# A decoder layer on one NeuronCore: values ahead of context pieces, head loads behind the stores, and the last attention batch in order of readiness

## The chip, the cores and the metric

The kernel runs on one core of a Trainium2 chip. The time is the device time of one execution in microseconds (us), a median over runs. The profile is one execution of the same kernel. The engines are TensorE (PE; its weight loads PEld), VectorE (DVE), ScalarE (ACT), GpSimd (POOL) and SyncE (SP), which here only issues the DMAs. Each engine runs its own instructions in program order and waits on semaphores.

## What is computed

One post-norm decoder layer, float32, for 8 batches of 128 rows with 512 columns (inputs `x`, a context of the same shape, and a mask):

```
x = layernorm(x + out(softmax(q k / 4 + alibi, causal) v))          # self-attention, 32 heads of 16
x = layernorm(x + wo(softmax(rope(q) rope(k) / sqrt(128) + mask) v)) # cross-attention, 32 query heads, 8 key/value heads of 128
x = layernorm(x + ffn(x))
ffn(x) = layernorm(relu(x up)^2 down + ((x fc1) expert fc2) * (sum of the 2 largest of x gate)) * gamma + beta
```

## The kernel before

**Precision.** Every float32 operand of a large product is split into a rounded part "hi" (a copy on ScalarE) and the rest "lo" (a subtraction, on GpSimd or VectorE), and `product` (L34) makes three matmul passes, hi·hi, hi·lo, lo·hi. A 128x512 tile with a contraction over 512 is 12 matmuls.

**Weights** come in pieces of 128x512 through a ring of five slots, `stage`: SyncE loads a slot (`Ring.load`), ScalarE makes hi (L162), GpSimd makes lo (L167), and the next load into that slot waits for that lo (`s_lo`).

**Four stages follow one another**, each with a function for each engine in steps `n`:

- `ProjectSelf` (A): 24 tiles in `order`: 16 query/key tiles ("qk", 0 to 15) and 8 value tiles ("v", 16 to 23), in four PSUM banks; a bank is free again when VectorE has added the bias into `val` (`s_val`). For each tile ScalarE makes hi (`s_vhi`) and GpSimd lo (`s_vlo`). SyncE stores the qk tiles in DRAM and loads them back by heads (`heads.load`, 12 DMAs for 16 heads of one batch). The same engines split the eight pieces of the transposed context `ctx` (numbers 20 to 27), one with each value tile: ScalarE `piece_hi` (L321), VectorE `piece_lo` (L378).
- `AttendSelf` (B): 64 steps of attention over four heads each, plus `STEPS - NS` = 7 steps that run the pipeline out. Beside it, steps 0 to 63 project the cross-attention's keys and values from the context into `kv_d` (`project`, with `pj` banks 6 and 7). For each batch there is a chain, the closing: weighted values in `ov` -> parts added (L837) -> times `rden` (L598, `s_o`) -> transposed on TensorE (L786) -> hi, lo (`oT`) -> output product (`close`, `s_y`) -> residual added (L866, `s_z`) -> `Rows.statistics` -> `Rows.root` and the normalisation (L108, L114, `s_row`) -> transposed (L122) -> hi (L132), lo (L137) into `xT`. `closing(n, lag, ends)` gives the batch that a part works on in step n; `ends` lists the steps for the last batches, 6 and 7. In the steps from 60 on, the first pieces of the cross-attention's weights (`NEXT_LOAD`, `NEXT_SPLIT`; 0 to 3 query weights, 4 to 7 `wo`) and the first four query tiles (`QUERY`, `ROTATE`) are worked in.
- `AttendCross` (C): 64 steps. Step n projects and rotates query tile n+5, computes scores n, transposes n-2, outputs n-3 and values n-2. The rotation is three VectorE instructions (`rotate`, L1098 to L1100), a sum on GpSimd (L1161), a hi on ScalarE (L976), a lo on GpSimd (L1169).
- `FeedForward` (D): its weight pieces are split within C's steps 58 to 64 (`SPLIT`), the two `lat` tiles (expert times fc2) are made at step `LAT`, and `x` of batch b gets statistics, normalisation (GpSimd, L114) and transposes at steps 59+b, 60+b, 61+b. From step `FIRST` = 65 on the `up` tiles begin.

The order of each engine's work is written out by hand; nothing reorders it.

## Time and profile before

| | |
|---|---|
| median of 3 runs | 978.54 us (976.09 to 979.15) |
| the profiled execution | 979.14 us; its span 977.4 us |
| TensorE busy in the span | 911.4 us (93%) |
| VectorE, GpSimd, ScalarE busy | 672.1, 526.4, 499.5 us |
| mean granted TensorE clock | 0.975 of 2.4 GHz |

The span runs from the first to the last instruction; the other 1.7 us of the execution lie around it. A share of busy time is a mean over stages with different limits, so the stages' borders have to be looked at by themselves.

### The profile page before, as it was taken

To read this page: it belongs to the slowest core of one execution; us is meant where nothing else is said; L and a number is where in the kernel's file an instruction comes from. 1 tells how busy PE (TensorE), PEld (TensorE's weight loads), DVE (VectorE), ACT (ScalarE), POOL (GpSimd) and SP (SyncE) were. 2 spreads that over 40 slices of the span, in tenths; PEclk is the share of its full clock that TensorE was granted. 3 is DMA by queue.
4 is the path that set the end of the run, shared out by engine and by line. 5 is a ranking of instruction groups with operands and counts; after the bars stand their busy time and mean duration, and the time that the engine had idled before them with its cause. 6 is when DMAs were issued, how large, how long until landed. Compare 5 with 4: busy or idle time off the path is not lost.

```text
span 977.4 us, 15760 instructions
## 1 busy us (share of the span) xinstructions
PE 911.4 (93%) x4812; PEld 772.1 (79%) x4812; DVE 672.1 (69%) x2163; ACT 499.5 (51%) x1565; POOL 526.4 (54%) x446
## 2 busy tenths in 40 slices
PE   7994999999999677999999999999999998999996
PEld 6873888888888556888888888888888887787885
DVE  5444777777777446777777777777777776665646
ACT  4324977776777215545554555455545554450220
POOL 4534753353235556666666666666666677655101
PEclk9997999999999878999999999999999998999999
DMA  8794995585454521113031121312113112110001
GB/s 273 232 234 129 220 181 148 135 156 133 132 130 141 197 94 33 33 36 127 33 119 37 53 107 33 122 41 79 73 36 127 34 35 85 55 33 22 22 6 38
DMA packets 68371, 96.65 MB, mean 99 GB/s; under 512 B 7232, under 2 KB 44352, under 8 KB 67264
## 3 DMA queue, kind: packets, MB, share of 16 engines
q1 hardware_dynamic: 68288, 95.65, 34.3%
q8 instruction: 39, 0.64, 0.3%
q14 instruction: 44, 0.36, 0.2%
HBM read 68.33 MB, written 27.26 MB: 98 GB/s over the span
## 4 chain that ended last, share of the span: by engine, by line
PE 77%; issue 6%; ACT 5%; DVE 5%; POOL 4%; SPq 1%; DMA 1%; POOLq 0%; ACTq 0%; DVEq 0%
PE banks L34 60%; PE banks L1055 4%; PE banks L1035 3%; PE banks L778 3%; PE banks L737 2%; ACT B_prob L663 2%; PE banks L736 2%; PE banks L1056 2%; SPq L209 1%; PE banks L766 1%; POOL x L1571 1%; PE banks L122 1%; POOL C_t L1161 1%; DMA stage<-ctxT_dram 1%; DVE A_val L392 1%
## 5 line engine op out<-in xcount | busy, mean ns | idle before, releaser
L34 PE MATMUL banks<-C_wo,C_o 128*128 128x512 f32 x768 | 191.4, 398 | 1.6 <-DVE C_o L1148 1.0
L34 PE MATMUL banks<-xT,C_w 128*128 128x512 f32 x768 | 191.0, 399 | 1.5 <-DVE xT L137 1.5
L34 PEld LDWEIGHTS banks<-xT,C_w 128*128 128x128 f32 x768 | 148.2, 194 | 33.2 <-issue 1.9
L34 PEld LDWEIGHTS banks<-C_wo,C_o 128*128 128x128 f32 x768 | 140.4, 189 | 29.7 <-issue 1.2
L976 ACT ACTIVATE C_q<-C_t 128x512 fp32r<-128x512 f32 x64 | 40.5, 633 | 175.6 <-POOL C_t L1161 175.6
L663 ACT ACTIVATE B_prob<-B_prob,B_top 128x128 f32<-128x128 f32 x256 | 99.5, 392 | 33.4 <-DVE B_top L816 32.5
L1169 POOL TENSOR_TENSOR C_q<-C_t,C_q 128x512 fp32r<-128x512 f32 x64 | 82.7, 1293 | 47.6 <-ACT C_q L976 47.6
L985 ACT ACTIVATE C_prob<-C_prob,C_top 128x128 f32<-128x128 f32 x256 | 99.0, 392 | 2.4 <-DVE C_top L1119 2.4
L1161 POOL TENSOR_TENSOR C_t<-C_t,C_t 128x512 f32<-128x512 f32 x64 | 82.8, 1294 | 13.6 <-DVE C_t L1100 13.4
L1055 PE MATMUL banks<-C_kv,C_q 128*128 128x256 f32 x256 | 68.8, 346 | 4.1 <-issue 3.7
L167 POOL TENSOR_TENSOR C_wo<-stage,C_wo 128x512 fp32r<-128x512 f32 x32 | 41.1, 1285 | 56.6 <-ACT C_wo L162 56.6
L1177 POOL TENSOR_TENSOR C_prob<-C_prob,C_rden 128x512 f32<-128x512 f32 x64 | 66.6, 1041 | 8.4 <-DVE C_rden L1130 8.4
L167 POOL TENSOR_TENSOR C_w<-stage,C_w 128x512 fp32r<-128x512 f32 x32 | 41.2, 1286 | 54.5 <-ACT C_w L162 54.5
L816 DVE CUSTOM_DVE_ANT_0 B_prob<-banks,causal 128x128 f32<-128x128 f32 x256 | 58.9, 287 | 12.0 <-issue 11.2
L1002 ACT ACTIVATE C_o<-banks 128x512 fp32r<-128x512 f32 x64 | 38.3, 599 | 53.5 <-PE banks L34 53.5
L1098 DVE TENSOR_TENSOR C_t<-banks,trig 128x512 f32<-128x512 f32 x64 | 44.2, 691 | 28.8 <-PE banks L34 28.7
L1148 DVE TENSOR_TENSOR C_o<-banks,C_o 128x512 fp32r<-128x512 f32 x64 | 44.3, 692 | 26.9 <-ACT C_o L1002 26.9
L822 DVE TENSOR_TENSOR B_pT<-banks,B_pT 128x512 fp32r<-128x512 f32 x64 | 44.1, 689 | 24.2 <-ACT B_pT L646 24.1
L1119 DVE CUSTOM_DVE_ANT_0 C_prob<-banks,C_prob 128x128 f32<-128x128 f32 x256 | 58.9, 286 | 2.7
L34 PE MATMUL banks<-C_pT,C_kv 128*128 128x512 f32 x192 | 54.8, 394 | 5.4 <-DVE C_pT L1137 5.0
L737 PE MATMUL banks<-vhl,B_pT 128*128 128x16 f32 x256 | 59.2, 256 | 0.0
L1056 PE MATMUL banks<-C_kv,C_q 128*128 128x128 f32 x256 | 57.6, 225 | 0.0
(154 smaller groups left out, 2137.0 us busy)
## 6 DMA issues: line engine op xcount, KB each, us to landing
C_kv<-cross_kv_d SPq DMA_DIRECT2D x8, 2048.0 KB, 8.5
cross_kv_d<-B_k_out SPq DMA_DIRECT2D x16, 512.0 KB, 2.7
cross_kv_d<-B_v_out SPq DMA_DIRECT2D x16, 512.0 KB, 4.1
stage<-wq_dram SPq DMA_DIRECT2D x32, 256.0 KB, 2.6
stage<-wo_dram SPq DMA_DIRECT2D x32, 256.0 KB, 2.6
heads_q<-heads_q_d SPq DMA_DIRECT2D x96, 64.0 KB, 4.0
heads_k<-heads_k_d SPq DMA_DIRECT2D x96, 64.0 KB, 4.1
heads_q_d<-cT SPq DMA_DIRECT2D x8, 512.0 KB, 2.6
```

The source lines that it names most:

```text
L34: mm = eng.matmul(out, stationary[i], moving[j], start=first and n == 0, stop=last and n == len(PASSES) - 1)
L167: eng.tensor_tensor(out, self.stage[:, n % self.SLOTS, :], hi.bitcast(F32), ALU.subtract).then_inc(self.s_lo, 1)
L663: last = eng.activation(e, e, ACT.Exp, bias=self.top[:, n % 4, h:h + 1], scale=-1.0, accum_out=self.total[:, HG * G + h:HG * G + h + 1])
L737: mm = eng.matmul(out[:, at:at + DH], self.pT[1][:, m % 2, h * S:(h + 1) * S], v[:, 0:DH], start=False, stop=True)
L816: last = eng.tensor_tensor_reduce(self.prob[:, n % 3, h * S:(h + 1) * S], self.sc[n % 2][:, h * S:(h + 1) * S], self.heads.causal, 1.0, 3e ...
L985: last = eng.activation(e, e, ACT.Exp, bias=self.top[:, n % 2, h:h + 1], scale=-1.0, accum_out=self.total[:, n % 2, h:h + 1])
L1055: eng.matmul(out, q[0][:, h, tok], both, start=True, stop=False)
L1056: mm = eng.matmul(out[:, 0:S], q[1][:, h, tok], both[:, 0:S], start=False, stop=True)
L1119: last = eng.tensor_tensor_reduce(self.prob[:, n % 2, h * S:(h + 1) * S], self.sc[:, h // 2, h % 2, 0, :], self.prob[:, n % 2, h * S:(h + ...
L1161: eng.tensor_tensor(t1, t1, t2, ALU.add).then_inc(self.s_sum, 1)
L1169: eng.tensor_tensor(self.query(r, 1), by_batch(self.t1[:, r % 2, :]), self.query(r, 0).bitcast(F32), ALU.subtract).then_inc(self.s_qlo, 1)
L1177: eng.tensor_tensor(e, e, self.rden[:, (n - 1) % 2, :].unsqueeze(2).broadcast_to([P, self.Q, S]), ALU.mult).then_inc(self.s_norm, 1)
```

## The change

It has four groups of edits.

1. **Values ahead of context pieces.** For a value tile, VectorE now adds the bias and ScalarE makes hi before the context piece of that tile is split, and not behind it. TensorE's first step of B and the first key projection no longer wait for all 24 `val`; only the first value projection (f == 1) does.
2. **Heads loads behind the stores.** Batch 0's head loads, which stood behind the stores of tiles 10 and 12, stand behind the last store; context pieces 20 to 23 are loaded behind the stores of tiles 9, 11, 13 and 15, pieces 24 to 27 between the two head loads.
3. **The last batch in order of readiness.** From step 65 on VectorE has its own list, `vector_end`. `root` is called by itself; the normalisation of batches 6 and 7 and the last scaling by `rden` move from GpSimd to VectorE. Several `ends` are one step earlier. Pieces 4 to 7 of the cross-attention's weights are split at step 70, behind all the rest of B, and `EARLY` is 9 (pieces 9 and 10 are loaded by C). In C's steps 0 to 2 the query projection stands ahead of the value product.
4. **Feed-forward pieces one step forward.** `SPLIT` begins at step 57, `LAT` is 59.

The diff, cut to its core (the bodies of `minima`, `turned_lo`, `add_parts`, `output_lo` and `add_row` are the old pieces of `vector` as functions):

```diff
@@ -109,7 +109,6 @@
 
     def normalise(self, eng, b):
 
-        self.root(eng, b)
         eng.wait_ge(self.s_rstd, b + 1)
         eng.tensor_scalar(self.x[:, b, :], self.x[:, b, :], self.moments[:, b, 0:1], self.rstd[:, b:b + 1],
                           ALU.subtract, ALU.mult).then_inc(self.s_row, 1)
...
-    HEADS = (10, 12)
 
     pieces = [(kind, c, 0) for c in range(C) for kind in ("x", "w")] + \
...
             heads.store(eng, i, m, h, self.tiles[i % heads.RING])
-            if i in self.HEADS:
-                heads.wait_stored(eng, self.QK // 2)
-                heads.load(eng, 0, self.HEADS.index(i))
-            if i >= self.QK - C:
-                self.load_piece(eng, self.CONTEXT + i - self.QK + C)
+            if i >= self.QK // 2 and i % 2 == 1:
+                self.load_piece(eng, self.CONTEXT + (i - self.QK // 2) // 2)
+        heads.wait_stored(eng, self.QK // 2)
+        heads.load(eng, 0, 0)
         for n in range(self.CONTEXT + C, len(self.pieces)):
             self.load_piece(eng, n)
+        heads.load(eng, 0, 1)
         for n in range(Ring.SLOTS):
             eng.wait_ge(self.s_lo, max(j for j in range(len(self.pieces)) if j % self.RING == n) + 1)
             ring.load(eng, n, sources[n])
@@ -322,9 +320,10 @@
 
     def scalar_tile(self, eng, i):
 
-        for n in self.pieces_with(i):
-            self.piece_hi(eng, n)
         kind, m, h = self.order[i]
+        if kind == "qk":
+            for n in self.pieces_with(i):
+                self.piece_hi(eng, n)
         eng.wait_ge(self.s_val, i + 1)
         src = self.val[:, i % 2, :]
...
             src = src.rearrange("p (h d) -> p h d", d=DH)
         eng.activation(dst, src, ACT.Copy).then_inc(self.s_vhi, 1)
+        if kind == "v":
+            for n in self.pieces_with(i):
+                self.piece_hi(eng, n)
 
     def scalar(self, eng):
 
...
@@ -380,9 +382,10 @@
 
     def vector_tile(self, eng, i):
 
-        for n in self.pieces_with(i):
-            self.piece_lo(eng, n)
         kind, m, h = self.order[i]
+        if kind == "qk":
+            for n in self.pieces_with(i):
+                self.piece_lo(eng, n)
         eng.wait_ge(self.s_acc, i + 1)
...
         else:
             eng.tensor_scalar(out, acc, self.bqk[:, m:m + 1], None, ALU.add).then_inc(self.s_val, 1)
+        if kind == "v":
+            for n in self.pieces_with(i):
+                self.piece_lo(eng, n)
 
     def vector(self, eng):
 
...
 
-    NEXT_LOAD = {57: range(5), 62: (5, 6), 64: (7,), 67: (8,), 68: (9,), 69: (10,)}
-    NEXT_SPLIT = {60: 0, 61: 1, 62: 2, 65: 3, 66: 4, 67: 5, 68: 6, 69: 7}
+    NEXT_LOAD = {57: range(5), 62: (5, 6), 64: (7,), 67: (8,)}
+    NEXT_SPLIT = {60: (0,), 61: (1,), 62: (2,), 65: (3,), 70: (4, 5, 6, 7)}
     QUERY = {64: 0, 65: 1, 66: 2, 67: 3}
     ROTATE = {65: 0, 66: 1, 67: 2, 68: 3}
 
...
-        return self.closing(n, 8 + 4 * half, ((56, 64), (60, 67))[half])
+        return self.closing(n, 8 + 4 * half, ((56, 64), (60, 66))[half])
...
+    def scale(self, eng, b, half):
+
+        done = 2 * b + half + 1
+        wait(eng, self.s_o, done - 1)
+        eng.wait_ge(self.s_oadd, done)
+        eng.wait_ge(self.s_rden, done)
+        o = self.o[:, 16 * half:16 * half + 16, :]
+        eng.tensor_tensor(o, o, self.rden[:, 16 * half:16 * half + 16].unsqueeze(2).broadcast_to([P, 16, DH]),
+                          ALU.mult).then_inc(self.s_o, 1)
+
 
     def gpsimd_pieces(self, eng, n):
 
@@ -590,22 +606,19 @@
 
         for half in range(2):
             b = self.half_of(n, half)
-            if b is not None:
-                done = 2 * b + half + 1
-                eng.wait_ge(self.s_oadd, done)
-                eng.wait_ge(self.s_rden, done)
-                o = self.o[:, 16 * half:16 * half + 16, :]
-                eng.tensor_tensor(o, o, self.rden[:, 16 * half:16 * half + 16].unsqueeze(2).broadcast_to([P, 16, DH]),
-                                  ALU.mult).then_inc(self.s_o, 1)
+            if b is not None and n <= self.NS:
+                self.scale(eng, b, half)
         j = self.tile("k", n, 2)
         if j is not None:
             eng.wait_ge(self.s_khi, j + 1)
             out = self.k_out[j % 2]
             eng.tensor_tensor(out[:, :, 1, :], by_batch(self.t1[j % 2][:, :]), out[:, :, 0, :].bitcast(F32),
                               ALU.subtract).then_inc(self.s_klo, 1)
-        b = self.closing(n, 19, (65, 69))
+        b = self.closing(n, 19, (64, 69))
         if b is not None:
-            self.rows.normalise(eng, b)
+            self.rows.root(eng, b)
+            if n < self.NS:
+                self.rows.normalise(eng, b)
         j = self.tile("k", n, 1)
         if j is not None:
             eng.wait_ge(self.s_cos, j + 1)
...
             eng.wait_ge(self.s_x[b], 16)
             eng.tensor_tensor(self.x1[:, b, :], self.x1[:, b, :], self.bout[:, :], ALU.add).then_inc(self.s_xadd, 1)
-        if n in self.NEXT_SPLIT:
-            self.cross.piece_lo(eng, self.NEXT_SPLIT[n])
+        for i in self.NEXT_SPLIT.get(n, ()):
+            self.cross.piece_lo(eng, i)
         if n in self.ROTATE:
             self.cross.tile_sum(eng, self.ROTATE[n])
             self.cross.tile_lo(eng, self.ROTATE[n])
...
             eng.activation(self.pT[0][:, n % 2, :], self.tp, ACT.Copy).then_inc(self.s_phi, 1)
-        b = self.closing(n, 21, (66, 70))
+        b = self.closing(n, 21, (65, 70))
         if b is not None:
             self.rows.hi(eng, b)
...
             eng.activation(self.k_out[j % 2][:, :, 0, :], by_batch(self.t1[j % 2][:, :]), ACT.Copy).then_inc(self.s_khi, 1)
         self.scalar_pieces(eng, n)
-        if n in self.NEXT_SPLIT:
-            i = self.NEXT_SPLIT[n]
+        for i in self.NEXT_SPLIT.get(n, ()):
             if i == 3:
...
         if part == 0:
-            if f < 2:
+            if f == 1:
                 eng.wait_ge(self.before.s_val, len(self.before.order))
-            else:
+            elif f > 1:
...
             if n == 0:
-                eng.wait_ge(self.before.s_val, len(self.before.order))
...
             mm.then_inc(self.s_ot, 1)
-        b = self.closing(n, 20, (66, 69))
+        b = self.closing(n, 20, (65, 69))
         if b is not None:
             if b == B - 1:
...
-        b = self.closing(n, 18, (65, 69))
+        b = self.closing(n, 18, (64, 69))
         if b is not None:
-            eng.wait_ge(self.s_y, b + 1)
-            eng.wait_ge(self.s_xadd, b + 1)
-            row = self.x1[:, b, :]
-            eng.tensor_tensor(row, self.yb, row, ALU.add).then_inc(self.s_z, 1)
-            eng.wait_ge(self.s_z, b + 1)
-            self.rows.statistics(eng, b)
-        if n in self.ROTATE:
-            if self.ROTATE[n] == 0:
-                for s in (self.s_klo, self.s_vlo):
-                    eng.wait_ge(s, len(self.FILL) // 2)
-            self.cross.rotate(eng, self.ROTATE[n])
+            self.add_row(eng, b)
+
+    def vector_end(self, eng):
+
+
+
+        first, last = B - 2, B - 1
+        self.rows.normalise(eng, first)
+        for s in (self.s_klo, self.s_vlo):
+            eng.wait_ge(s, len(self.FILL) // 2)
+        self.cross.rotate(eng, 0)
+        self.turned_lo(eng, self.NS - 1)
+        self.rows.lo(eng, first)
+        self.cross.rotate(eng, 1)
+        self.add_parts(eng, last, 1)
+        self.scale(eng, last, 1)
+        self.output_lo(eng, last)
+        self.cross.rotate(eng, 2)
+        self.cross.rotate(eng, 3)
+        self.add_row(eng, last)
+        self.rows.normalise(eng, last)
+        self.rows.lo(eng, last)
 
 
 class AttendCross:
...
     PIECES = 2 * HG * NG
-    EARLY = 11
+    EARLY = 9
     STEPS = NS + 3
...
-    SPLIT = {58: (0, 1), 59: (2, 3), 60: (4, 5), 61: (6, 7), 62: (8, 9), 63: (10, 11), 64: (12,)}
+    SPLIT = {57: (0, 1), 58: (2, 3), 59: (4, 5), 60: (6, 7), 61: (8, 9), 62: (10, 11), 63: (12,)}
     DOWN = 13
     STATS, NORMAL, TURN, TAKE = 59, 60, 61, 62
-    LAT = 60
+    LAT = 59
     FIRST = 65
 
     tiles = [("lat", l, 0) for l in range(L)] + \
...
         if self.NORMAL <= n < self.NORMAL + B:
+            self.rows.root(eng, n - self.NORMAL)
             self.rows.normalise(eng, n - self.NORMAL)
         for i in self.SPLIT.get(n, ()):
             self.piece_lo(eng, i)
...
         for n in range(self.before.STEPS, self.NORMAL + B):
+            self.rows.root(eng, n - self.NORMAL)
             self.rows.normalise(eng, n - self.NORMAL)
         for m in range(self.M):
...
                 d.tensor_between(eng, n)
+                if n < 3:
+                    c.queries(eng, n)
                 c.values(eng, n)
-                c.queries(eng, n)
+                if n >= 3:
+                    c.queries(eng, n)
                 d.tensor_behind(eng, n)
             d.tensor(eng)
 
         @block.vector
         def _(eng):
             a.vector(eng)
-            for n in range(b.STEPS):
+            for n in range(b.NS + 1):
                 b.vector(eng, n)
+            b.vector_end(eng)
             for n in range(c.STEPS):
                 d.vector_ahead(eng, n)
                 c.vector(eng, n)
...
```

## Rows read from the trace of the kernel before

**Rows 1.** Busy time of each engine in four stretches, with granted clock and DMA share
```profile
77.00:87.00 10.00, 0.37 (x3) 0.10 (x1) 6.20 (x7) 3.57 (x7) 3.80 (x3) 0.73 0.27 79
...
333.00:353.00 20.00, 11.78 (x41) 9.36 (x41) 7.80 (x14) 4.42 (x9) 13.26 (x11) 0.70 0.46 166
...
373.00:795.00 422.00, 422.00 (x2185) 357.86 (x2184) 325.43 (x1008) 218.27 (x674) 270.07 (x224) 1.00 0.19 65
795.00:845.00 50.00, 43.50 (x219) 36.10 (x218) 34.81 (x111) 26.48 (x80) 41.15 (x34) 0.93 0.27 80
```

**Rows 2.** Timeline at the end of A: start, us, engine, line, operation, count, idle before
```profile
54.65 9.13 PE L34 MATMUL banks<-A_w,A_xT 128*128 128x512 f32 x39 [0.24 <-DVE A_w L378]
...
56.65 0.43 SPq L275 DMA_DIRECT2D stage<-ctxT_dram  x1
...
62.66 0.63 ACT L321 ACTIVATE cT<-stage 128x512 fp32r<-128x512 f32 x1 [6.74 <-DMA stage<-ctxT_dram]
...
63.94 0.68 DVE L392 TENSOR_TENSOR A_val<-banks,A_bv 128x512 f32<-128x512 f32 x1
...
65.84 1.38 DVE L378 TENSOR_TENSOR cT<-A_rest,cT 128x512 fp32r<-128x512 f32 x1 [1.22 <-ACT cT L321]
...
86.17 0.68 DVE L392 TENSOR_TENSOR A_val<-banks,A_bv 128x512 f32<-128x512 f32 x1
...
86.90 0.80 PE L766 MATMUL banks<-heads_k,heads_q 128*128 128x256 f32 x2 [9.63 <-DVE A_val L392]
90.22 2.90 PE L34 MATMUL banks<-cT,B_wk 128*128 128x512 f32 x6 [2.53 <-POOL B_wk L167]
```

**Rows 3.** Timeline of TensorE from the end of B into C
```profile
325.54 0.63 PE L122 MATMUL banks<-ident,x 128*128 128x128 f32 x4 [1.57 <-issue]
...
335.10 1.11 PE L786 MATMUL banks<-ident,B_o 128*128 128x128 f32 x4 [6.19 <-POOL B_o L598]
335.87 5.39 PE L34 MATMUL banks<-xT,C_w 128*128 128x512 f32 x12
...
347.62 0.36 PE L1055 MATMUL banks<-C_kv,C_q 128*128 128x256 f32 x1 [3.65 <-issue]
...
352.92 8.16 PE L34 MATMUL banks<-xT,C_w 128*128 128x512 f32 x24 [1.50 <-DVE xT L137]
...
371.46 1.62 PE L34 MATMUL banks<-C_pT,C_kv 128*128 128x512 f32 x3 [4.95 <-DVE C_pT L1137]
```

**Rows 4.** Timeline of GpSimd in the same stretch
```profile
346.25 1.27 POOL L1169 TENSOR_TENSOR C_q<-C_t,C_q 128x512 fp32r<-128x512 f32 x1 [0.74 <-ACT C_q L976]
...
348.14 2.08 POOL L114 TENSOR_SCALAR x<-x,first_moments,first_rstd 128x512 f32<-128x512 f32 x1
```

**Rows 5.** The page's costliest groups: count, then busy us, mean ns of one
```profile
L976 ACT ACTIVATE C_q<-C_t 128x512 fp32r<-128x512 f32 x64 | 40.5, 633 | 175.6 <-POOL C_t L1161 175.6
...
L1169 POOL TENSOR_TENSOR C_q<-C_t,C_q 128x512 fp32r<-128x512 f32 x64 | 82.7, 1293 | 47.6 <-ACT C_q L976 47.6
...
L1161 POOL TENSOR_TENSOR C_t<-C_t,C_t 128x512 f32<-128x512 f32 x64 | 82.8, 1294 | 13.6 <-DVE C_t L1100 13.4
...
L1177 POOL TENSOR_TENSOR C_prob<-C_prob,C_rden 128x512 f32<-128x512 f32 x64 | 66.6, 1041 | 8.4 <-DVE C_rden L1130 8.4
...
L1098 DVE TENSOR_TENSOR C_t<-banks,trig 128x512 f32<-128x512 f32 x64 | 44.2, 691 | 28.8 <-PE banks L34 28.7
```

**Rows 6.** Groups by shape, VectorE: a normalisation of D as VectorE does it
```profile
L1513 DVE TENSOR_SCALAR x<-x,D_moments,D_rstd 128x512 f32<-128x512 f32 x8 | 4.4, 546 | 5.3 <-POOL D_rstd L1574 5.3
```

**Rows 7.** Timeline of TensorE where C runs out and D begins
```profile
819.89 1.11 PE L122 MATMUL banks<-ident,x 128*128 128x128 f32 x4 [4.02 <-DVE D_lat L1466]
...
823.25 4.12 PE L34 MATMUL banks<-C_wo,C_o 128*128 128x512 f32 x12
...
835.90 2.97 PE L34 MATMUL banks<-C_wo,C_o 128*128 128x512 f32 x12 [1.03 <-DVE C_o L1148]
...
844.23 3.00 PE L34 MATMUL banks<-xT,D_up 128*128 128x512 f32 x12
```

More of the change, by code:

```diff
@@ L802, in tensor, with minima, turned_lo, add_parts @@
             self.cross.project(eng, self.QUERY[n])
+    def minima(self, eng, n):
+        if n == 0:
+            eng.wait_ge(self.heads.s_causal, 2)
+        eng.wait_ge(self.s_sc, n + 1)
+        wait(eng, self.s_tp, n - 2)
+        wait(eng, self.s_exp, n - 3)
+        eng.memset(self.carrier[:, n:n + 1], 0.0)
+        for h in range(HG):
+            last = eng.tensor_tensor_reduce(
+                self.prob[:, n % 3, h * S:(h + 1) * S], self.sc[n % 2][:, h * S:(h + 1) * S],
+                self.heads.causal, 1.0, 3e38, ALU.add, ALU.min, self.top[:, n % 4, h:h + 1])
+        last.then_inc(self.s_top, 1)
+    def turned_lo(self, eng, m):
+        eng.wait_ge(self.s_phi, m + 1)
+        eng.tensor_tensor(self.pT[1][:, m % 2, :], self.tp, self.pT[0][:, m % 2, :].bitcast(F32),
+                          ALU.subtract).then_inc(self.s_plo, 1)
+    def add_parts(self, eng, b, half):
+        o = self.o[:, 16 * half:16 * half + 16, :]
+        eng.wait_ge(self.s_olow, 2 * b + half + 1)
+        eng.tensor_tensor(o, self.values_of(half)[:, :, 0, :], o, ALU.add).then_inc(self.s_oadd, 1)
+    def output_lo(self, eng, b):
+        eng.wait_ge(self.s_ohi, b + 1)
+        eng.tensor_tensor(self.oT[1][:, :, :], self.ot.rearrange("p (c s) -> p c s", c=C),
+                          self.oT[0][:, :, :].bitcast(F32), ALU.subtract).then_inc(self.s_olo, 1)
+    def add_row(self, eng, b):
+        eng.wait_ge(self.s_y, b + 1)
+        eng.wait_ge(self.s_xadd, b + 1)
+        row = self.x1[:, b, :]
+        eng.tensor_tensor(row, self.yb, row, ALU.add).then_inc(self.s_z, 1)
+        eng.wait_ge(self.s_z, b + 1)
+        self.rows.statistics(eng, b)
     def vector(self, eng, n):
@@ L808, in vector @@
         if self.live(n):
[L809 to L819 removed]
+            self.minima(eng, n)
         if self.live(n, self.LT):
[L821 to L824 removed]
+            self.turned_lo(eng, n - self.LT)
+        b = self.closing(n, 21, ())
         if b is not None:
@@ L834, in vector @@
             if b is not None:
[L835 to L837 removed]
+                self.add_parts(eng, b, half)
         b = self.closing(n, 15, (63, 67))
         if b is not None:
[L840 to L842 removed]
+            self.output_lo(eng, b)
         cos, sin = (self.trig[:, 2 + i, :].unsqueeze(1).broadcast_to([P, 4, S]) for i in range(2))
```

21 lines of the change are left out of this document (removed).

## The prediction

> **What bounds the kernel now.** I read the windows first. Through C's steady part TensorE is busy 422.0 of 422.0 us at the full clock [rows 1], so nothing can be won there. What can be won lies at the borders of stages: 9.6 of 10 us idle at the end of A, 8.2 of 20 at the end of B at a mean clock of 0.70, and 6.5 of 50 at 0.93 where C runs out [rows 1]. The timeline then says what ends each wait. End of A: TensorE has done its last value tile at 77.27 (86.90 less 9.63) and waits for the last `val` on VectorE; then 2.53 us more for the first key weight [rows 2]. End of B: 6.19 us for the scaled output of batch 7, 3.65 us ahead of the first scores, 1.50 us for the last transposed row, 4.95 us for the first value product [rows 3]. Each long gap is followed by slow work: a projection of 12 matmuls takes 5.39 us at 335.87 [rows 3], and the stream of 39 in 9.13 us at 54.65 [rows 2] makes 2.7 to 2.8 of it; that is the lower of the two clocks, 1.2 instead of 2.4 GHz. C to D: 4.02 us for `lat` [rows 7].
>
> **Part 1, end of A.** VectorE is the bound: its `val` of the first value tile comes at 63.94, because ScalarE had to wait until 62.66 for a context piece whose load was issued at 56.65, behind the head loads; the eighth `val` comes at 86.17 [rows 2]. So a tile costs (86.17 - 63.94)/7 = 3.18 us, and TensorE needs only 2.7. The cycle is `val` 0.68, hi 0.63, piece hi about 0.6, piece lo 1.38 [rows 2], and each waits for the one before. Turning the order round doesn't shorten it: the same four stand in the same circle. What it does is let it start: the first value tile is complete about 55.4 (54.65 plus three matmuls), and its `val` needs no context any more. First `val` 55.5, eighth 55.5 + 7 x 3.18 = 77.7 instead of 86.17: 8.5 us earlier. Behind the eighth there is now a last piece lo, up to 81.0; the key weight's hi follows the last piece hi at about 79.7 and GpSimd's lo ends about 81.7, where it ended just ahead of 90.22 [rows 2]. So the first key projection starts at 81.8 and not 90.2: 8.4 us. The first scores move ahead to 74.9 and wait for nothing but their heads. Against this stand the loads: SyncE now issues piece 23, twelve head loads, pieces 24 to 27 and twelve more behind the last store at 57.3. In before a piece issued at 56.65 was in use 6.0 us later, in just such a queue [rows 2]. Piece 24 would be issued about 64 and arrive about 70 to 71.5; the cycle wants it at 69.5. Lower bound of the gain: 2 us late there and 1 us for the key weight, 5.4 us; upper bound 8.5. I take 7.5, one microsecond late. The batch's second heads are wanted only four steps later. The low clock at the first steps of B costs now as before, since TensorE still idles nearly 7 us.
>
> **Part 2, end of B.** I walk the chain with the durations of [rows 4, 5, 6]. The normalisation of batch 6 moves to VectorE (0.55 us [rows 6] instead of 2.08 [rows 4]) and comes right behind its output product, so that its transposes stand one step earlier and TensorE runs through without the gap of 1.57 us ahead of its transposes: it has the third query tile done at 327.3 instead of 328.9 (335.10 less 6.19 [rows 3]). Meanwhile the last parts are added and scaled on VectorE behind the second rotation (about 325.1 + 0.4 + 0.4), so the output transposes find their input at 326.0: the 6.19 us go, and the fourth query tile runs at the full clock, 2.7 for 5.39. The output product of batch 7 ends about 333.3, not 344.0 (347.62 less 3.65 [rows 3]). What is late next is the rotations: VectorE does the third and fourth behind `output_lo` (329.3), 3 x 0.7 each, to 333.5; the residual and statistics follow to 335.4. GpSimd and ScalarE need 1.29 + 0.63 + 1.29 and some 0.1 for hand-overs, 3.3 us a tile, for tiles 2 and 3: 331.4 + 6.7 = 338.1 [rows 5]; that lo ended at 347.52 before (346.25 + 1.27 [rows 4]). Then root 0.6 (347.52 to 348.14) and normalisation 0.55 to 339.3 (350.22 before [rows 4]), while the scores run from 338.1; transposes, hi and lo put C's first projection at 342.4 against 352.92 [rows 3]: 10.5 us. TensorE idles nearly 5 us ahead of the scores, so I let the pair of projections cost the 8.16 us that it cost [rows 3], at the low clock in its first half. In C's step 2 the fourth projection, 2.7 us, now stands in the 4.95 us gap ahead of the value product, and neither is slowed by it (the product took 1.62 us for three matmuls [rows 3]); after taking off 1.2 us that the next value product waits for its own lo, this adds 2.3. Sum 12.8, of which I take 12.5. The four splits of `wo` at step 70 occupy GpSimd for 4 x 1.29 = 5.2 us from about 342.3 to 347.5, and the sum of the fifth query tile is ready about then: hidden, but without slack; if it loses, 1 to 2 us. Bounds: below, 8 (one more wait of 2 us in VectorE's single file, and the low clock over one more projection, 2.7); above, 14.5 (the clock stays up ahead of C, which takes 2.7 off the pair of projections, less what the chain then waits for).
>
> Two vector operations of two SBUF inputs or in a fast mode now run beside GpSimd. The piece lo takes 1.38 us at 65.84 beside GpSimd and 0.69 without it [rows 2] (the multiplication of as many elements shows the 0.69 [rows 5]). I take 0.3 us for the scaling and nothing for the normalisations, since GpSimd has nothing to do at those moments. The Trainium skill (SBUF — State Buffer, Who interferes with whom) says why: VectorE in a two-port mode or with two SBUF inputs and a reading GpSimd shut each other out for a whole instruction. By that rule each of three moved instructions could wait or hold up a full GpSimd instruction, and part 2 would give some 3 us less; the trace agrees about the piece lo and can't show the moved ones.
>
> **Part 3, C to D.** The third piece that `lat` needs was split at step 59; at step 58 GpSimd has the same two-piece room. `lat` (12 matmuls, 2.7 us) then stands at step 59 and its hi and lo are done by about 815.1 instead of 819.8, when TensorE gets to the first transposes of the second norm: the 4.02 us go [rows 7]. So does the low clock behind them: the output product took 4.12 us for 2.97 [rows 7], and a mean clock of 0.93 over 50 us [rows 1] is 3.5 us of lost clock, of which I put 0.8 into the idle time and 2.7 into work. The later steps are held by GpSimd, which has 1.04 [rows 5] + 0.6 + 2.08 [rows 4] + 2 x 1.29 = 6.3 us a step while pieces last, and TensorE has about 5.3; the pieces now end a step earlier, so that the waits there, 1.03 before 835.90 [rows 7] and the rest of the 6.5 us idle [rows 1], can go too. 6.5 + 2.7 = 9.2; the first `up` tile would start at 835 and not 844.23. I take 8.5; lower bound 4 (one wait comes back and the clock falls again), upper 9.2. From there to the end the order is the old one and TensorE sets it: the gain stays.
>
> **Sum.** 7.5 + 12.5 + 8.5 = 28.5 us. The profiled execution's own 979.14 less this is 950.6; the median shown is 0.6 lower, so 950.0.
>
> **Rivals.** *The tail of B stays at the low clock* or VectorE's single file (`vector_end` puts some ten jobs in one fixed order) meets a wait that I don't see, or each of its three moved instructions loses a GpSimd instruction of 1.3 us as the piece lo does [rows 2]. For it: gaps of 3.65 us and more were each followed by slow matmuls [rows 3], and the new gap is nearly 5. Against: the biggest gap is gone. Part 2 gives 5: 957. The Trainium skill (TensorE: Matmul & The Clock Gate, What's actually happening) says that the slow state is the default and activity releases it; the trace agrees [rows 3]. *The loads decide at the end of A*: context piece 24 or the key weight comes 5 us late behind 24 head loads. Part 1 gives 2: 955.5. *C to D is held by GpSimd all the same*, as its 6.3 us a step suggest; part 3 gives 3: 955.5. *The change does nothing where it counts*: the first part's circle of four is as long as before, and if TensorE at the start of B were held by the weights' arrival in every case, part 1 gives 0 and the others half: 968; still faster. *The other side*: TensorE falls to 1.2 GHz over whole stretches of the transitions because the small gaps now follow one another. Each slow 12-matmul tile costs 2.7 us more [rows 3], so it decides once 28.5/2.7, some 11, are slow beyond those that are slow now. From B's step 64 to C's step 2 there are ten (eight queries, two output products), about three of them slow now, and C's last steps hold six more. The trace shows no stretch of dense work that stays slow, so 2 in 100.
>
> **How the numbers follow.** The forecast 0.60, with its own range of 946 to 955. Part 2 short 0.15, loads 0.09, GpSimd in part 3 0.10, little or nothing 0.04, slower 0.02. The range takes in the two bounds that are added (upper 8.5 + 14.5 + 9.2 = 32.2, so 946; lower 5.4 + 8 + 4 = 17.4, so 961). A difference under 0.3% (2.9 us) is about what a measurement of this kernel can't tell from none. Faster 0.95, same 0.02, slower 0.03.
>
> **What would show it.** Right: the first key projection at about 82 to 83 with a gap of some 7 us ahead; the output transposes of batch 7 without a gap, C's first projection about 18 us earlier than 352.92 and C's steady part about 20 us earlier; the gap before the first D transpose gone, the first `up` tile 28 us earlier, clock 1.00 there. Wrong: a wait of ScalarE for a context piece over 2 us, the first scores of B waiting for heads, more than 6 us idle on TensorE ahead of C's first scores, a clock of 0.5 in C's steps 2 and 3, or GpSimd releasing the first transposes of D.

## The result and the profile after

The changed kernel takes 953.81 us (median of 4 runs, 952.4 to 954.57) beside 978.85 for the kernel before on the same chip: ratio 0.9748, 95% interval 0.9726 to 0.977, so 25.0 us less. Forecast were 950.0, with bounds that give 946 to 961. The profiled executions differ by more, 952.4 and 979.14, 26.7 us. One execution of the same code is not the next: in three traces with the same A (before, tail_only and ff_only below) the first value product starts at 54.65, 54.18 and 54.75, and the first key projection 35.6, 34.6 and 34.6 us behind it. The one microsecond more in the trace of before is ScalarE's wait for the first context piece: 6.74 us there, 5.81 and 5.75 in the other two. So I compare marks within a trace and take whole runs for the verdicts.

The windows of the changed kernel: stretch, length, busy us of TensorE, its weight loads, VectorE, ScalarE and GpSimd, then granted clock, DMA share, GB/s.

```profile
76.00:84.00 8.00, 0.77 (x2) 0.71 (x3) 4.38 (x13) 3.97 (x11) 4.20 (x3) 0.71 0.65 134
326.00:336.00 10.00, 3.75 (x14) 3.27 (x15) 4.13 (x13) 3.12 (x7) 5.46 (x5) 0.63 0.07 29
336.00:346.00 10.00, 10.00 (x43) 8.07 (x41) 6.14 (x21) 2.55 (x10) 6.98 (x7) 0.86 0.32 107
360.00:776.00 416.00, 416.00 (x2157) 352.91 (x2156) 322.63 (x1002) 217.05 (x672) 270.57 (x224) 1.00 0.19 67
776.00:818.00 42.00, 38.79 (x209) 32.00 (x208) 33.11 (x108) 23.76 (x72) 37.12 (x31) 1.00 0.27 83
```

C's steady part is as full as before [rows 1]; what changed are the borders. At the end of B two gaps are left, 4.79 and 1.50 us, with a mean clock of 0.63 in the ten microseconds around them, and where C runs out 3.2 us are idle in place of 6.5.

The timeline at the end of A, to be laid beside [rows 2]:

```profile
56.25 0.69 DVE L395 TENSOR_TENSOR A_val<-banks,A_bv 128x512 f32<-128x512 f32 x1 [0.40 <-PE banks L34]
...
63.52 0.63 ACT L336 ACTIVATE vhl<-A_val 128x512 fp32r<-128x512 f32 x1 [2.04 <-DVE A_val L395]
64.06 0.62 ACT L319 ACTIVATE cT<-A_rest 128x512 fp32r<-128x512 f32 x1
...
64.71 1.37 DVE L380 TENSOR_TENSOR cT<-A_rest,cT 128x512 fp32r<-128x512 f32 x1 [1.22 <-ACT cT L319]
66.00 0.68 DVE L395 TENSOR_TENSOR A_val<-banks,A_bv 128x512 f32<-128x512 f32 x1
...
78.72 0.68 DVE L395 TENSOR_TENSOR A_val<-banks,A_bv 128x512 f32<-128x512 f32 x1
...
83.23 2.90 PE L34 MATMUL banks<-cT,B_wk 128*128 128x512 f32 x6 [7.73 <-POOL B_wk L166]
```

The first bias waits for TensorE alone; from there on bias, copy of the value, copy of the piece, low part and next bias follow one another every 3.2 us, none of them behind a DMA.

TensorE from the end of B into C, beside [rows 3]:

```profile
319.87 0.60 PE L797 MATMUL banks<-ident,B_o 128*128 128x128 f32 x4
320.23 3.01 PE L34 MATMUL banks<-xT,C_w 128*128 128x512 f32 x12
323.08 2.88 PE L34 MATMUL banks<-B_wout,B_oT 128*128 128x512 f32 x12
330.75 0.55 PE L1102 MATMUL banks<-C_kv,C_q 128*128 128x256 f32 x1 [4.79 <-issue]
...
335.06 7.44 PE L34 MATMUL banks<-xT,C_w 128*128 128x512 f32 x24 [1.50 <-DVE xT L136]
...
347.82 2.98 PE L34 MATMUL banks<-xT,C_w 128*128 128x512 f32 x12
352.93 0.93 PE L34 MATMUL banks<-C_pT,C_kv 128*128 128x512 f32 x3 [2.14 <-DVE C_pT L1184]
```

The 6.19 us are gone, the fourth query tile takes 3.01 and not 5.39. GpSimd in the same stretch, beside [rows 4], shows what is late next:

```profile
329.39 1.26 POOL L1216 TENSOR_TENSOR C_q<-C_t,C_q 128x512 fp32r<-128x512 f32 x1 [0.74 <-ACT C_q L1023]
330.61 0.55 POOL L108 TENSOR_TENSOR first_rstd<-first_moments,power 128x1 f32<-128x1 f32 x1
```

TensorE where C runs out, beside [rows 7]:

```profile
794.77 0.94 PE L34 MATMUL banks<-C_pT,C_kv 128*128 128x512 f32 x3 [1.05 <-ACT C_pT L1041]
...
800.82 0.93 PE L34 MATMUL banks<-C_pT,C_kv 128*128 128x512 f32 x3 [0.22 <-issue]
...
809.17 3.00 PE L34 MATMUL banks<-C_wo,C_o 128*128 128x512 f32 x12 [0.98 <-DVE C_o L1195]
...
814.32 3.01 PE L34 MATMUL banks<-C_wo,C_o 128*128 128x512 f32 x12 [0.59 <-issue]
...
817.52 3.00 PE L34 MATMUL banks<-xT,D_up 128*128 128x512 f32 x12
```

The 4.02 us and the slow output product are gone, but the 1.03 and 0.59 us of before stand as 0.98 and 0.59, and 1.05 us at 794.77 is new.

The same end of C, from the transposes of step 59 to the first `up` tile, in the trace before, in the changed kernel and in the run `piece_copies_behind` below:

```profile
797.86:844.23 46.37, 39.87 (x203) 33.15 (x202) 32.80 (x107) 23.95 (x71) 37.52 (x32) 0.93 0.28 82
776.81:817.52 40.71, 37.50 (x203) 30.96 (x202) 32.45 (x107) 22.95 (x69) 35.83 (x30) 1.00 0.28 85
775.95:814.97 39.02, 37.32 (x203) 30.92 (x202) 32.14 (x107) 23.32 (x69) 34.82 (x30) 1.00 0.29 89
```

TensorE's idle time (length less its busy time) goes from 6.50 to 3.21 us, its busy time from 39.87 to 37.50.

From these marks the 26.7 us divide: up to B's last scores (307.31 before, 300.12 after) 7.2; from there to the transposes of C's step 59 (797.86 and 776.81) 13.9; from there to the first `up` tile (46.37 and 40.71) 5.7.

### The profile page after: what moved, and what is told of

Same layout as the page of the kernel before. It is cut to its first block, busy times and chain, and to the rows that moved or that the text cites. A ratio compares the mean times of both kernels' runs of the same rounds, so it can differ in the third digit from the quotient of the medians.

```text
span 950.6 us, 15757 instructions
## 1 busy us (share of the span) xinstructions
PE 901.9 (95%) x4812; PEld 765.9 (81%) x4812; DVE 673.7 (71%) x2166; ACT 498.4 (52%) x1565; POOL 522.3 (55%) x443
## 4 chain that ended last, share of the span: by engine, by line
PE 79%; ACT 6%; issue 6%; DVE 6%; POOL 2%; DMA 0%; POOLq 0%; ACTq 0%; DVEq 0%
PE banks L34 61%; PE banks L1102 4%; PE banks L1082 3%; PE banks L789 3%; PE banks L749 2%; ACT B_prob L676 2%; PE banks L748 2%; PE banks L1103 2%; PE banks L777 1%; POOL x L1620 1%; PE banks L121 1%; ACT C_prob L1032 1%; DVE A_val L395 1%; ACT cT L319 0%; DVE B_prob L825 0%
## 5 line engine op out<-in xcount | busy, mean ns | idle before, releaser
L34 PE MATMUL banks<-xT,C_w 128*128 128x512 f32 x768 | 186.9, 393 | 1.5 <-DVE xT L136 1.5
L34 PEld LDWEIGHTS banks<-xT,C_w 128*128 128x128 f32 x768 | 145.0, 190 | 32.0 <-issue 1.9
L34 PE MATMUL banks<-cT,B_wk 128*128 128x512 f32 x192 | 52.4, 409 | 7.9 <-POOL B_wk L166 7.7
```

The costliest lines, as they stand in the source:

```text
L34: mm = eng.matmul(out, stationary[i], moving[j], start=first and n == 0, stop=last and n == len(PASSES) - 1)
```

## Experiments

Each run was measured beside the kernel before on its own chip, whose median was 978.4 to 978.9 us; the ratios are to that. The edits are shown shortened, with words in brackets for code left out.

### Each part alone, on the kernel before

`loads_only` takes over the order of the loads alone (group 2 of the change):

```diff
@@ ProjectSelf.sync @@
-            if i in self.HEADS: (wait, heads.load)
-            if i >= self.QK - C: self.load_piece(...)
+            if i >= self.QK // 2 and i % 2 == 1:
+                self.load_piece(eng, self.CONTEXT + (i - self.QK // 2) // 2)
+        heads.load(eng, 0, 0); pieces 24 to 27; heads.load(eng, 0, 1)
```

> The kernel before with the order of the loads alone changed: pieces 20 to 23 go out between the last eight stores, the loads of the heads behind the stores, the rest between the two. Theory one, the order of the loads carries most of part 1: the value tile waited for late context pieces, and with them earlier the last value tile comes at about 80.2 us and the first k projection at about 84.2 instead of 90.22, so about 6 us off. Rival, the order of the work carries it: each piece is still split ahead of its value tile, so the chain of piece, value tile, piece stays as it was and under 2 us come off.

972.86 us, ratio 0.9943 (0.9928 to 0.9958), 5.6 us. Its first key projection starts at 84.17, forecast 84.2.

`order_only` has the other half, values ahead of pieces and the loosened waits:

```diff
@@ ProjectSelf.scalar_tile and vector_tile @@
-        for n in self.pieces_with(i): piece        # ahead of the bias or copy, for every tile
+        (that for "qk" tiles; for "v" tiles the same loop behind it)
```

> The kernel before with only the order of work at the end of A changed (value tile ahead of its context piece on ScalarE and VectorE, and the waits of the first scores and projections on the value tiles loosened); the loads stay as before. Theory one: a piece that lands late still holds the value tile behind it, so about 3 us come off, and loads and order together (7.2) are less than the sum of each alone (6 + 3). Rival, the order carries it: 6 to 7 us.

976.15 us, 0.9975 (0.9964 to 0.9986), 2.4 us by the runs; the key projection comes at 85.90. VectorE's biases, and ScalarE's copy of the first piece between them:

```profile
55.46 0.69 DVE L397 TENSOR_TENSOR A_val<-banks,A_bv 128x512 f32<-128x512 f32 x1 [0.39 <-PE banks L34]
...
61.02 0.63 ACT L321 ACTIVATE cT<-stage 128x512 fp32r<-128x512 f32 x1 [4.20 <-DMA stage<-ctxT_dram]
...
62.29 0.69 DVE L397 TENSOR_TENSOR A_val<-banks,A_bv 128x512 f32<-128x512 f32 x1
```

The first bias is early, the second comes 6.8 us later, behind the first piece, whose copy on ScalarE waited for its load. So it is the loads that carry most of part 1, and the two halves share one wait. Counted from the first value product to the first key projection it is 34.6 us in tail_only and ff_only, 31.4 with the order alone, 29.6 with the loads alone and 28.0 with both: 3.2, 5.0 and 6.6 us off.

`tail_only` is the third group of edits alone (separate `root`, `vector_end`, steps 64 to 70, `wo` at step 70, queries first in C's steps 0 to 2).

> The kernel before with the end of B alone changed (the last batch in order of readiness, steps 64 to 70, and the queries of C's first three steps ahead of the values). From the two traces part 2 is 13.9 us; if the parts are independent this run is 13.9 off (ratio 0.9858). Rival, a share of it was the earlier arrival of loads or a clock that part 1 set: 12 or less. The first projection of C at about 342 in this trace.

964.29 us, 0.9855 (0.984 to 0.987), 14.2 us. From B's last scores to C's first projection it takes 34.99 us, the changed kernel 34.94, before 45.61. In this trace the end of B needs nothing of the other parts.

`ff_only` is `SPLIT` and `LAT` alone, the fourth group.

> The kernel before with the feed-forward pieces and the latent tiles one step forward and nothing else. If the parts add, 5.7 us come off (ratio 0.9942), as between the traces of before and after. Rival, the forecast's 8.5 was right and 2.8 of it was eaten by an interplay with the other parts: then 8.5 here. In the trace, TensorE still waits for C_pT and C_o in steps 61 to 64.

974.05 us, 0.995 (0.9935 to 0.9965), 4.9 us; from step 59's transposes to the first `up` tile 40.72 us, the changed kernel's 40.71. So the 2.8 us that the forecast had more weren't lost to the other parts. The four ratios added make 27.1 us, and the whole change, by its ratio, 24.7; what is left between them is the overlap of the first two. By the runs the order adds nothing to the loads that can be told (24.7 less 14.2 and 4.9 is 5.6, as much as the loads alone); by the marks above it adds 1.6.

### Parts of the end of B, on the changed kernel

`no_swap`:

```diff
-                if n < 3: c.queries(eng, n)
                 c.values(eng, n)
-                if n >= 3: c.queries(eng, n)
+                c.queries(eng, n)
```

> The changed kernel with the queries of C's steps 0 to 2 behind the values again. Theory: the values of steps 2 wait for the split of the transposed probabilities, and the projection that stands ahead of them covers that wait; without it TensorE stands still and the rotation of the next query tile starts later: 2.3 to 3.2 us slower than the changed kernel (about 956.5). Rival: GpSimd's file of rotations, splits and normalisations sets the steps there, and the place of the projection on TensorE changes nothing (953.8).

956.09 us, 0.9776 (0.9761 to 0.9792), 2.7 us more than the changed kernel by the ratios, whose intervals just touch; in the trace the stretch from C's first projection to the first `up` tile is 485.85 us for 482.46, 3.4 more. The old wait is back, with its low clock:

```profile
353.26 1.62 PE L34 MATMUL banks<-C_pT,C_kv 128*128 128x512 f32 x3 [4.95 <-DVE C_pT L1184]
354.68 5.08 PE L34 MATMUL banks<-xT,C_w 128*128 128x512 f32 x12
```

The swap is worth part of the wait that it covers (2.14 us of it are left) and the slow projection behind it: by the trace more than the forecast's 2.3.

`spread` splits `wo` one a step again, and with it loads pieces 9 and 10 in B again (`NEXT_LOAD` and `EARLY` as before the change):

```diff
-    NEXT_SPLIT = {60: (0,), 61: (1,), 62: (2,), 65: (3,), 70: (4, 5, 6, 7)}
+    NEXT_SPLIT = {60: (0,), 61: (1,), 62: (2,), 65: (3,), 66: (4,), 67: (5,), 68: (6,), 69: (7,)}
```

> The changed kernel with the four output weights of C split one a step in steps 66 to 69 again, as before the change, in place of all four in step 70. Theory: four low parts of 1.26 us stand in GpSimd's file among the sums and low parts of the queries, of which 2 to 4 us fall on the way to the first scores (330.75): 2.5 to 4 us slower than the changed kernel. Rival: GpSimd's gaps of 0.74 to 2.00 us between its rotations hold them, since it waits for the copy on ScalarE and the rotation on VectorE: under 1 us.

954.56 us, 0.9761 (0.9746 to 0.9775): by the runs not to be told from the changed kernel. In the trace the first scores come 33.10 us behind B's last scores, in place of 30.63, so 2.5 us late, and all of it arrives at the first `up` tile (2.7); its opening of A happened to be 0.8 us earlier. The trace speaks for the theory, the runs leave anything from nothing to some 3 us, and the two later loads aren't told apart from the splits.

`root_first` takes up the two rows of GpSimd above: the root's input is there at 327.98 (VectorE's last step of the statistics ends then), but it stands behind the low part of query tile 3.

```diff
             self.cross.tile_sum(eng, self.ROTATE[n])
+            if self.ROTATE[n] == 3: self.rows.root(eng, B - 1)
             self.cross.tile_lo(eng, self.ROTATE[n])
@@ AttendSelf.tensor @@
-            if b == B - 1: self.cross.scores(eng, 0)
             eng.wait_ge(self.s_z, b + 1)
             self.rows.transpose(eng, b)
+            if b == B - 1: self.cross.scores(eng, 0)
```

> The changed kernel with the square root of the last row's variance ahead of the low part of query tile 3 in GpSimd's file (its input is there at 327.98, it ran at 330.61), and the transposes of that row ahead of C's first scores on TensorE. Theory: the row is normalised at about 329.2 in place of 331.19, its low part done at about 332.3 in place of 334.92, and C's first projection starts at about 332.6 in place of 335.06: 2.4 us faster (951.4). Rival: the projections of C's steps 0 to 2 wait for something else (the rotation, GpSimd) and catch nothing: under 0.5 us.

949.26 us, 0.9705 (0.969 to 0.972). From B's last scores to C's first projection 32.62 us, 2.3 less, and 0.5 more behind it: 2.9 us in the trace, 4.2 by the ratios of the runs. The edit has two halves, and the rows of the changed kernel show that the root alone could not have done it: there the row is normalised at 331.74 (VectorE from 331.19, 0.55), but the transposes stand behind the scores, which fill TensorE until 332.49.

```profile
331.19 0.55 DVE L113 TENSOR_SCALAR x<-x,first_moments,first_rstd 128x512 f32<-128x512 f32 x1 [3.21 <-POOL first_rstd L108]
...
332.49 1.07 PE L121 MATMUL banks<-ident,x 128*128 128x128 f32 x4
```

In `root_first` they start at 330.06, the scores run behind them, and the pair of projections waits for nothing. What each half is worth alone wasn't run.

`warm` fills TensorE's two gaps with products that nothing reads:

```diff
+        if n == 0: (30 products heads_q x heads_k, 128x512, into the bank of the first projection)
+            if b == B - 1: (20 products of xT, 128x512, into a free bank, ahead of C's first scores)
```

> The changed kernel with products added that nothing reads, in the two gaps of TensorE's: 30 of 512 columns ahead of B's first k projection, 20 ahead of C's first scores. Theory: the granted clock stays at its upper level where the rows show the lower one (0.50 in 80 to 86 and in 330 to 338), the scores, transposes and first projections behind the gaps run in half the time, and some 3.4 us at the end of B and 1.5 us at the end of A come off. Rival: what stands behind the gaps waits for VectorE, ScalarE and GpSimd again, and the faster products only make longer waits: under 1 us together.

948.94 us, 0.9695 (0.9673 to 0.9718): by the ratios 5.2 us less than the changed kernel, give or take 3, and 2.6 between the two profiled executions, which is what the marks divide. By the marks: the key projection starts at 83.22 as before and takes 1.62 us for six matmuls in place of 2.90, B's last scores come 1.3 us earlier; at the end of B it is 1.0 to C's first projection and 0.3 behind it. That is 1.3 for the 1.5 expected at A and 1.3 for the 3.4 at B. The windows show why:

```profile
330.00:331.00 1.00, 1.00 (x10) 0.90 (x9) 0.52 (x1) 0.00 (x0) 0.00 (x0) 1.00 0.00 0
331.00:332.00 1.00, 0.25 (x3) 0.01 (x1) 0.08 (x1) 0.71 (x2) 0.00 (x0) 1.00 0.00 0
332.00:333.00 1.00, 0.24 (x1) 0.28 (x2) 1.00 (x3) 1.00 (x3) 0.52 (x1) 0.68 0.00 0
333.00:334.00 1.00, 1.00 (x3) 0.81 (x4) 0.96 (x9) 0.96 (x2) 1.00 (x2) 0.50 0.00 0
```

The scores and transposes ran at the full clock, but the wait of 1.50 us for the last row's low part stayed, the clock fell within it (0.68 on the mean of the microsecond from 332, with the projections starting at 332.76), and the pair of projections took 7.13 us, nearly the 7.44 of the changed kernel.

### The end of A

`late_low_part` opens the circle:

```diff
@@ ProjectSelf.vector_tile @@
-        if kind == "v": low parts of pieces_with(i)
+        if kind == "v" and i > self.QK: low parts of pieces_with(i - 1)
@@ vector @@
+        (behind the loop: low parts of pieces_with of the last tile)
```

> The changed kernel with VectorE's low part of a context piece behind the bias of the next value tile, in place of ahead of it. Theory: the period of 3.19 us of the value tiles is a circle (bias on VectorE 0.68, copy of the value tile on ScalarE, copy of the piece, low part 1.37, next bias); broken, TensorE's 2.76 us a tile sets the period, the last bias comes at about 75.6 in place of 78.72 and B's first k projection at about 80.1 in place of 83.23: 3.1 us off. Rival: pieces 24 to 27 (issued 65.1 to 67.3, landed up to 73.8) hold it then, and about 1 us comes off.

951.19 us, 0.9723 (0.9696 to 0.975), which the runs alone don't tell from the changed kernel. The period is TensorE's 2.72 us, and the last bias comes at 74.64:

```profile
69.20 0.69 DVE L395 TENSOR_TENSOR A_val<-banks,A_bv 128x512 f32<-128x512 f32 x1 [1.43 <-PE banks L34]
70.08 0.69 DVE L380 TENSOR_TENSOR cT<-stage,cT 128x512 fp32r<-128x512 f32 x1 [0.18 <-ACT cT L319]
71.92 0.69 DVE L395 TENSOR_TENSOR A_val<-banks,A_bv 128x512 f32<-128x512 f32 x1 [1.15 <-PE banks L34]
...
76.55 1.34 DVE L380 TENSOR_TENSOR cT<-stage,cT 128x512 fp32r<-128x512 f32 x1 [0.62 <-ACT cT L319]
```

but the first key projection came at 81.31, only 1.3 us earlier when the 0.66 us of the earlier opening are taken off. SyncE and ScalarE say why:

```profile
73.40 0.43 SPq L156 DMA_DIRECT2D stage<-wk_dram  x1
...
79.19 0.63 ACT L161 ACTIVATE B_wk<-stage 128x512 fp32r<-128x512 f32 x1 [2.67 <-DMA stage<-wk_dram]
```

The key weight stood behind twelve head loads in SyncE's queue. It arrived after the last bias had long been done. A context piece was late too, as the rival had it (ScalarE waited 1.57 us for it at 69.41), but the biases kept their period. Neither theory had the weight: the circle was real, and right behind it stood another queue.

### Where C runs out

`light_pieces` takes GpSimd's work away:

```diff
@@ FeedForward.piece_lo, for the pieces ahead of `down` @@
-        self.ring.lo(eng, self.first + n, hi[:, :], lo[:, :])
+        (the same subtraction for one column; the products read hi in the place of lo)
```

> The changed kernel, with the low parts of the 13 feed-forward pieces of steps 57 to 63 left out: GpSimd computes one column of each, and the products read the high part twice (same work on TensorE, another result). That takes 13 x 1.25 = 16 us from GpSimd. Theory one, GpSimd's file of 6.2 us a step (normalise 793.43, 799.65, 805.86) holds steps 61 to 64: TensorE's idle 3.2 us between 776 and 818 goes down to about 1 and 2 to 2.5 us come off. Rival, the circle of values, output copy on ScalarE, low part on VectorE and outputs holds them: the waits of 0.98 for C_o at 809.17 and 0.59 at 814.32 stay, and under 0.5 us come off.

951.91 us, 0.9735 (0.9717 to 0.9752), which doesn't tell it from the changed kernel. The window is to be read beside the last one above:

```profile
776.00:818.00 42.00, 38.84 (x209) 32.00 (x208) 32.98 (x107) 22.73 (x68) 25.50 (x29) 1.00 0.24 79
```

GpSimd is busy 25.50 us for 37.12, TensorE stands as before: 40.71 us to the first `up` tile, to the hundredth. In the changed kernel its instructions stand back to back through most of these steps, and still it held nothing.

`piece_copies_behind` moves ScalarE's copies of the pieces:

```diff
@@ AttendCross.scalar @@
             eng.activation(self.pT[0][:, :], self.tp[n % 2], ACT.Copy).then_inc(self.s_phi, 1)
+        self.after.scalar_pieces(eng, n)          # was ahead of this step's work, in scalar_ahead
```

> The changed kernel with ScalarE's copies of the feed-forward pieces behind the copy of the transposed probabilities in steps 57 to 63, in place of ahead of it. light_pieces left steps 59 to 65 at 40.71 us with 16 us less work on GpSimd, so GpSimd does not hold them. Theory: ScalarE's file does; in step 61 the copy of C_pT starts at 793.36 behind 1.15 us of pieces, and TensorE waits 1.05 us for it. With the pieces behind it 1.5 to 2.5 us come off steps 61 to 64. Rival: the circle of values, output copy, low part and outputs holds them whatever stands ahead of the copy: under 0.5 us.

951.75 us, 0.9729 (0.9708 to 0.9751), which the runs don't tell from the changed kernel; in the trace 39.02 us to the first `up` tile in place of 40.71. The first two lines are of the changed kernel, where the copy of C_pT stood behind the pieces; in the others it is ahead of them:

```profile
792.32 1.15 ACT L161 ACTIVATE D_up<-stage 128x512 fp32r<-128x512 f32 x2
793.36 0.59 ACT L1041 ACTIVATE C_pT<-banks 128x512 fp32r<-128x512 f32 x1
...
791.46 0.60 ACT L1041 ACTIVATE C_pT<-banks 128x512 fp32r<-128x512 f32 x1
791.93 1.15 ACT L161 ACTIVATE D_up<-stage 128x512 fp32r<-128x512 f32 x2
```

The waits of 1.05, 0.98 and 0.59 us go; 1.70 us idle are left of 3.21. Only now GpSimd ends some of them, 1.13 us:

```profile
806.13 0.66 PE L1083 MATMUL banks<-ident,C_prob 128*128 128x128 f32 x4 [0.79 <-POOL C_prob L1225]
...
811.09 0.66 PE L1083 MATMUL banks<-ident,C_prob 128*128 128x128 f32 x4 [0.34 <-POOL C_prob L1225]
```

### A version that beats both

`together` joins them, with the key weight loaded ahead of the second heads and a few more unread products around the last transposes:

```diff
@@ ProjectSelf.sync @@
-        heads.load(eng, 0, 1)
         for n in range(Ring.SLOTS):
+            if n == 1: heads.load(eng, 0, 1)
```

> The changed kernel with what helped put together: the low part of a context piece behind the next bias, the last root first and the last row's transposes ahead of the scores, the piece copies behind the copy of C_pT, products that nothing reads in the gaps (16 ahead of B's first k projection, 15, 2 and 2 around the last transposes and C's first scores), and, new, B's first key weight loaded ahead of the twelve loads of the second heads (in late_low_part it was issued at 73.40 behind them and landed at 79.1, when the last bias had long been done). Theory, the gains of different places add: 1.3 (low part) + 2.7 (weight earlier, first k projection at about 79 for an opening of A as in the changed kernel) + 1.2 + 1.4 (clock at the two gaps) + 2.9 (root) + 1.7 (copies) = 11.2 off 953.8, so about 942.6. Rival: the gaps are used twice; with earlier arrivals the clock's share and the root's overlap, and 7 to 8 come off (946).

942.48 us (median of 5 runs, 941.54 to 943.37), ratio 0.9631 (0.9612 to 0.965) to before: 36.1 us, 11.3 more than the change alone. TensorE:

```profile
79.92 1.62 PE L34 MATMUL banks<-cT,B_wk 128*128 128x512 f32 x6 [0.72 <-POOL B_wk L166]
...
326.26 0.63 PE L121 MATMUL banks<-ident,x 128*128 128x128 f32 x4 [0.54 <-issue]
...
328.85 5.63 PE L34 MATMUL banks<-xT,C_w 128*128 128x512 f32 x24
```

The pair of projections takes 5.63 us for 24 matmuls with no wait ahead of it. Here the transposes stand ahead of the scores, unread products stand behind both, and the clock stays up. The key weight was issued at 71.47, for 73.40 in `late_low_part` and 73.96 in the changed kernel, and the key projection starts 3.3 us earlier than in the changed kernel, for openings of A that are equal to 0.05 us (first bias at 56.30 and 56.25).

## Why the prediction was right, and where its sizes were off

**Part 1, 7.5 forecast, 7.0 to 7.2 found.** The steps held: first bias at 56.25 (55.5), a period of 3.2 us that the new order doesn't shorten, key projection at 83.23 (81.8), of which 0.6 us is the later opening of this execution. From the first value product on it is 7.6 us less than in the trace of before and 6.6 less than in the two others with the same A, so the 7.5 is met within what one trace can say. The late context piece, the forecast's one microsecond, didn't come: ScalarE never waited for a piece. The forecast spoke of starting the circle early; `order_only` shows that the loads let it run.

**Part 2, 12.5 forecast, 13.9 found.** To C's first projection 10.7 us (10.5). In C's steps 0 to 3 it was 3.2 for the forecast's 2.3: `no_swap` shows that the swap alone is 3.4, because the slow projection behind the wait (5.08 for 2.98) goes with it. The pair of projections, taken at 8.16, took 7.44. The scaling on VectorE cost what was taken, 0.74 for 0.42 us, and GpSimd's sum beside it 1.47 for 1.29:

```profile
317.37 1.29 POOL L1216 TENSOR_TENSOR C_q<-C_t,C_q 128x512 fp32r<-128x512 f32 x1 [0.80 <-ACT C_q L1023]
317.69 0.42 DVE L840 TENSOR_TENSOR B_o<-banks,B_o 128x256 f32<-128x256 f32 x1
318.21 0.74 DVE L595 TENSOR_TENSOR B_o<-B_o,B_rden 128x256 f32<-128x256 f32 x1
318.62 1.47 POOL L1208 TENSOR_TENSOR C_t<-C_t,C_t 128x512 f32<-128x512 f32 x1
```

The Trainium skill (SBUF — State Buffer, Who interferes with whom) says that the one that issues first has the shared ports for its whole instruction and the other is blocked meanwhile. The rows agree: the scaling began 0.45 us before the end of GpSimd's low part and took 0.32 longer. So the moved instruction paid no more than the rest of the one under way (GpSimd's sum behind it paid 0.2), and the rival's 1.3 us for each was too much here. The low part of a context piece takes 1.37 us (64.71 in the changed kernel) and 1.34 (76.55 in `late_low_part`), where GpSimd's low part of the value had begun 0.5 us before it (64.23 and 76.07), and 0.69 where GpSimd's began only near its end (70.08 and 70.64, `late_low_part`).

**Part 3, 8.5 forecast, 5.7 found: the mis-sized term.** The forecast's 9.2 were 6.5 of idle time and 2.7 of work at the lower clock. The work gave 2.4 (39.87 to 37.50 busy), of the idle time only 3.3 went: the wait of 4.02 did, and a new one came. Wrong was "the later steps are held by GpSimd (...) the pieces now end a step earlier, so that the waits there, 1.03 before 835.90 [rows 7] and the rest of the 6.5 us idle [rows 1], can go too". They stayed, and one of 1.05 us came. GpSimd's 6.3 us a step were right as a sum and wrong as a bound (`light_pieces`). What held TensorE for half of the 3.2 us was ScalarE's order, the copies of pieces ahead of the copy of C_pT (`piece_copies_behind`, 1.7 us in the trace); of the 1.7 left there GpSimd ended 1.1, so it is next in line, but no run has both it and ScalarE out of the way. ScalarE's order is not new: in the trace before, the copies of the two `lat` tiles (817.93), of two pieces (821.53) and of C_pT (822.57) stand in the same order. There TensorE, 4.02 us late and at the lower clock behind it, wanted C_pT only at 827.21, and the order cost nothing.

**The rivals.** That the loads decide at A's end: no in this kernel, but yes as soon as the circle is open (`late_low_part`). That the tail stays at the low clock: the gap of nearly 5 us and 0.63 over ten us came as forecast, and cost no more than was in the sum. C to D held all the same: its 3 us lie as far below the 5.7 as the forecast lies above, and in the changed kernel the engine it named was the wrong one.

Shown by runs: the shares of the loads, the order, the tail and the feed-forward pieces; the root together with the transposes; the unread products; the swap, at the edge of the intervals. Shown by one trace each and not by the runs: the 2.5 us of the four `wo` splits and the two loads that went with them, the opened circle, ScalarE's order. Open: what holds the 4.79 us that are left ahead of C's first scores, beyond that GpSimd's low part of query tile 3 ends them; a shorter chain of rotation, sum, copy and low part wasn't tried.

## What to carry to other kernels

An engine that is nearly full is not thereby the bound: lay its file (its instructions in program order) beside the waits of the engine that counts, and ask of each wait which single instruction ended it and what stood ahead of that one in its own file. An order that cost nothing while a longer wait covered it becomes the next bound when that wait goes, so look at every engine for what stands ahead of the instruction that is wanted next. And behind the circle that was opened here stood another queue, so look up when the next input was issued before counting the gain.

## What the runs showed of the hardware

Filling a gap of TensorE's with unread products paid 1.3 us at each of two borders in the trace, and the work behind them started no later. But one gap left open was enough: with the gap of 4.8 us filled and one of 1.50 us left behind it (331.25 to 332.76), the granted clock was 0.68 in the microsecond from 332 and 0.50 in the next (`warm`). The Trainium skill (TensorE: Matmul & The Clock Gate, What's actually happening) says that activity releases the clock; the trace agrees, and adds that so short a wait was seen to lose it, while behind the waits of 1.36 us ahead of 91.51 in the changed kernel and of 1.00 us ahead of the key projection in `warm` the granted clock was still 1.00. Why the one and not the others, these runs don't show.
